# Delta loop over two steps with the next solve between halves of the chunk products, and 64 identity products ahead of it

## What is computed

```python
x = _layernorm(x + _L0_attn_ref(x, ...), axis=-1)   # delta rule
x = _layernorm(x + _L0_ffn_ref(x, ...), axis=-1)
x = _layernorm(x + _L1_attn_ref(x, ...), axis=-1)
x = _layernorm(x + _L1_ffn_ref(x, ...), axis=-1)

def step(S, xs):                                    # one chunk of one head
    qc, kc, vc, bc = xs
    kb = kc * bc[:, None]
    A = jnp.tril(kb @ kc.T, -1)
    U = solve_triangular(eye + A, vc * bc[:, None] - kb @ S, lower=True)
    o = qc @ S + jnp.tril(qc @ kc.T) @ U
    return (S + kc.T @ U, o)
```

## Time and profile before

| | us |
|---|---|
| median of 3 runs | 882.79 |
| lowest and highest | 877.17 and 887.01 |
| the profiled execution | 882.23 |
| its span, first to last instruction | 880.5 |

### The profile page before, as it was taken

One profiled execution on the slowest core, in us unless ns is written; L12 is line 12 of the kernel. 1 busy time (PEld: TensorE's weight loads), 2 busy tenths in 40 slices (PEclk: granted clock), 3 DMA queues, 4 the chain that ended last, 5 costly groups with the idle time before them and its releaser, 6 DMA issues. The chain is left out here.

```text
span 880.5 us, 38401 instructions
## 1 busy us (share of the span) xinstructions
PE 637.1 (72%) x15895; PEld 474.7 (54%) x15895; DVE 440.9 (50%) x1380; ACT 323.9 (37%) x743; POOL 330.2 (38%) x605
## 2 busy tenths in 40 slices
PE   5777105888886875368876189999832899999991
PEld 4565104777775774268876056767621354445551
DVE  3664350223232238826556036676538376776762
ACT  4554100122221213245554036455220556565651
POOL 3577302122121750345675654210021344646442
PEclk9888555599998577669999579999955899999995
DMA  3000222112210900544453111000005333333420
GB/s 104 8 15 21 79 86 69 38 66 71 72 65 22 330 26 1 99 137 131 152 158 106 48 38 28 17 4 4 4 1 99 101 98 100 108 99 106 100 83 1
DMA packets 62384, 63.72 MB, mean 72 GB/s; under 512 B 12432, under 2 KB 51903, under 8 KB 62017
## 3 DMA queue, kind: packets, MB, share of 16 engines
q1 hardware_dynamic: 57056, 52.35, 19.4%
q0 software_dynamic: 5216, 9.87, 5.3%
HBM read 20.50 MB, written 11.93 MB: 37 GB/s over the span
## 5 line engine op out<-in xcount | busy, mean ns | idle before, releaser
L1976 PE MATMUL e_psH<-wac,e_xT 128*64 x184 | 91.1, 618 | 1.0 <-ACT e_xT L2036 0.7
L1978 PE MATMUL e_psH<-e_up_w,e_xT 128*64 128x512 f32 x184 | 91.1, 618 | 0.0
L1921 POOL DMA_INDIRECT e_row<-xe_dram,e_read_at x46 | 44.6, 969 | 69.6 <-DVE spare L2167 44.3
L1926 POOL DMA_INDIRECT out<-spare,e_write_at x46 | 46.5, 1011 | 48.1 <-ACT spare L2053 37.8
L577 POOL TENSOR_TENSOR tb<-tinv,mb 128x128 f32<-128x128 f32 x64 | 24.3, 401 | 106.8 <-PE d_psY L594 106.8
L1321 ACT ACTIVATE e_hT<-e_psH,e_b 128x128 f32<-128x128 f32 x156 | 44.5, 369 | 39.2 <-PE e_psH L1277 39.2
L1233 POOL DMA_INDIRECT e_row<-xe_dram,e_read_at x39 | 38.7, 993 | 42.1 <-DVE spare L1392 27.7
L1277 PE MATMUL e_psH<-e_xT,e_up_w 128*128 128x128 f32 x312 | 45.5, 293 | 12.0 <-issue 9.9
L1997 PE MATMUL e_psY<-vb,e_hT 128*64 x368 | 50.9, 282 | 2.9 <-issue 2.9
L2160 DVE TENSOR_TENSOR e_h<-e_pre,e_psH 128x512 f32<-128x512 f32 x46 | 31.6, 688 | 42.4 <-ACT e_pre L2042 42.4
L2000 PE MATMUL e_psY<-e_down_w,e_hT 128*64 128x128 f32 x368 | 50.9, 282 | 0.0
(11 more groups left out here) (369 smaller groups left out, 1749.0 us busy)
## 6 DMA issues: line engine op xcount, KB each, us to landing
e_down_w<-vb SPq DMA_DIRECT2D x92, 128.0 KB, 2.0
e_up_w<-wa SPq DMA_DIRECT2D x39, 256.0 KB
xe_dram<-xe SPq DMA_DIRECT2D x2, 2080.0 KB, 12.4
vk_now<-vk SPq DMA_DIRECT2D x16, 192.0 KB
kq_now<-kq SPq DMA_DIRECT2D x16, 192.0 KB, 2.1
outs_dram<-spare SPq DMA_DIRECT2D x39, 64.0 KB
r<-in_L_attn_hidden_states SPq DMA_DIRECT2D x8, 256.0 KB, 3.1
gk_now<-gk SPq DMA_DIRECT2D x16, 128.0 KB, 2.0
```

The source lines that it names most:

```text
L1921: pool.indirect_dma_start(out=row[g % ROWS][:, :], out_offset=None, in_=x_dram, in_offset=bass.IndirectOffsetOnAxis(ap=read_at[:, g:g + 1] ...
L1926: pool.indirect_dma_start(out=out, out_offset=bass.IndirectOffsetOnAxis(ap=write_at[:, g:g + 1], axis=0), in_=z[:, g], in_offset=None, bou ...
L1976: nc.tensor.matmul(psH[g % 2][0:HALF, j], xT[g % 2][:, 0:HALF], wac[:, bass.ds(who[0][j], 1)].rearrange("p a f -> p (a f)"), start=True, s ...
L1978: mm = nc.tensor.matmul(psH[g % 2][HALF:P, j], xT[g % 2][:, HALF:P], up_w[g % 2][j][:, :], start=True, stop=True)
```

## The change

PE's loop now covers two steps in a pass, with buffers by the parity of the step, and has 7 passes. A step starts the solve of the step after it: the three bursts of the solve of t + 1 and the serial chain of t - 1 stand between the two halves (one sequence each) of the chunk products of t. `scan` is split into `states` and `outputs`, and the outputs are issued one place later. There are six identity products a step instead of nine. Step 0 and half of step 1's solve stand ahead of the loop, the rest of step 14, step 15 and its scan behind it. `mt`, `qe` and `kq_now` have two buffers, and the two banks psY and psZ become `psY[0]` and `psY[1]`; `across` writes to the bank that `first` has written, after ACT's copy. 24 identity products stand at the start of the delta stage, 40 at the end of the inversion's PE list, after a wait for `turned`, which counts the inversion's last two copies.

```diff
@@ stage_invert, PE
                 mm.then_inc(l_ps, 1)
+                pe.wait_ge(turned, SU)
+                half_words = sb["ident"][:, :].bitcast(BF16)[:, 0:P]
+                for i in range(40):
+                    nc.tensor.matmul(psW[:, i % 4], half_words, half_words, start=True, stop=True)
@@ stage_delta, buffers
-        vk_now, kq_now, gk_now = tmp("vk_now", [P, B * H, RW]), tmp("kq_now", [P, B * H, RW]), tmp("gk_now", [P, B * H, CH])
+        vk_now, gk_now = tmp("vk_now", [P, B * H, RW]), tmp("gk_now", [P, B * H, CH])
+        kq_now = [tmp(f"kq_now{i}", [P, B * H, RW]) for i in range(2)]
-        mt, qe = tmp("mt", [P, NC, B, CH]), tmp("qe", [P, B, NC, CH])
+        mt, qe = ([tmp(f"{n}{i}", s) for i in range(2)] for n, s in (("mt", [P, NC, B, CH]), ("qe", [P, B, NC, CH])))
-        solved_in, crossed_in = bank("d_psY", [P, 512]), bank("d_psZ", [P, 512])
+        solve = [bank(f"d_psY{i}", [P, 512]) for i in range(2)]
@@ stage_delta, SP
-                    if t:
-                        sp.wait_ge(c_ps, t)
+                    if t >= 2:
+                        sp.wait_ge(c_ps, t - 1)
@@ stage_delta, PE
+                def step(t, i, loads):
+
+                    j = 1 - i
+                    first(t + 1, j)
+                    states(t - 1, 0, j)
+                    per_chunk(t, 0, i, loads)
+                    full_array(rest[i])
+                    outputs(t - 1, 0, j)
+                    states(t - 1, 1, j)
+                    across(t + 1, j)
+                    outputs(t - 1, 1, j)
+                    states(t - 1, 2, j)
+                    per_chunk(t, 1, i)
+                    outputs(t - 1, 2, j)
+                    states(t - 1, 3, j)
+                    full_array(rest[i])
+                    second(t + 1, j)
+                    outputs(t - 1, 3, j)
-                pe.wait_ge(const, 3)
-                first(0, True)
-                across(0)
-                second(0)
-                per_chunk(0, True)
-                with pe.Fori(1, PER) as t:
-                    first(t, False)
-                    scan(t - 1, 0)
-                    full_array(rest[1])
-                    across(t)
-                    scan(t - 1, 1)
-                    full_array(rest[0])
-                    second(t)
-                    scan(t - 1, 2)
-                    full_array(rest[1])
-                    scan(t - 1, 3)
-                    per_chunk(t, False)
+                for _ in range(8):
+                    full_array(rest[1])
+                pe.wait_ge(const, 1)
+                first(0, 0, True)
...
+                with pe.Fori(0, PER // 2 - 1) as m:
+                    step(2 * m + 1, 1, 16 * m + 16)
+                    step(2 * m + 2, 0, 16 * m + 32)
...
@@ stage_delta, ACT
+                solved(0)
+                crossed(0)
+                for t in range(PER):
+                    if t + 1 < PER:
+                        solved(t + 1)
+                        crossed(t + 1)
+                    own(t)
@@ stage_delta, DVE
+                for t in range(PER + 1):
+                    if t < PER:
+                        remainders(t)
+                    if t >= 2:
+                        outputs(t - 2)
...
```

More of the change, by code:

```diff
@@ L568, in _ @@
                 pool.memset(S[:, 0], 0.0).then_inc(const, 1)
-                pool.memset(mt[:, :, :, :], 0.0).then_inc(const, 1)
+                for i in range(2):
+                    pool.memset(mt[i][:, :, :, :], 0.0).then_inc(const, 1)
                 pool.memset(uw[:, :], 0.0).then_inc(const, 1)
@@ L587, in full_array @@
                     for _ in range(3):
-                        nc.tensor.matmul(bank[:, :], half_words, half_words, start=True, stop=True)
+                        nc.tensor.matmul(bank, half_words, half_words, start=True, stop=True)
                 def apply(i, right, out, done):
@@ L611, in across, with second @@
                         for c in range(NC):
-                            mm = nc.tensor.matmul(psZ[row(c), bh], gk_now[key(c), bh], y0[key(c), bh * RW:(bh + 1) * RW], start=True, stop=True)
+                            mm = nc.tensor.matmul(psY[i][row(c), bh], gk_now[key(c), bh], y0[key(c), bh * RW:(bh + 1) * RW], start=True, stop=True)
                     mm.then_inc(z_ps, 1)
-                def second(t):
+                def second(t, i):
                     pe.wait_ge(expanded[1], t + 1)
@@ L618, in second @@
                     pe.sem_inc(passed, 1)
[L619 to L642, removed]
@@ L644, in scan, with per_chunk @@
-                def scan(t, c):
+                    apply(1, lambda bh: zz[:, bh * RW:(bh + 1) * RW], psY[i], w_ps)
+                def per_chunk(t, b, i, loads=0, start=False):
+                    if b == 0:
+                        pe.wait_ge(kq_in[i], loads)
+                        if not start:
+                            pe.wait_ge(on_done, t)
+                            pe.wait_ge(mt_done, t)
+                            pe.wait_ge(qe_done, t)
+                        pe.wait_ge(uw_done, t + 1)
+                        pe.sem_inc(passed, 1)
+                    for h in range(H):
+                        bh, at = b * H + h, (b * H + h) * RW
+                        for c in range(NC):
+                            nc.tensor.matmul(psC[row(h), c, b * P:b * P + RW], uw[row(c), at + DV:at + DV + CH], kq_now[i][row(c), bh],
+                                             start=True, stop=True)
+                        for c in range(NC):
+                            nc.tensor.matmul(psC[row(h), c, b * P + RW + CH:b * P + RW + 2 * CH], uw[row(c), at:at + DV], kq_now[i][row(c), bh, DK:RW],
+                                             start=True, stop=True)
+                        for c in range(NC):
+                            mm = nc.tensor.matmul(psC[row(h), c, b * P + RW:b * P + RW + CH], kq_now[i][row(c), bh, 0:CH], uw[row(c), at:at + DV],
+                                                  start=True, stop=True)
+                    if b == B - 1:
+                        mm.then_inc(c_ps, 1)
@@ L646, in scan, with states @@
+                def states(t, c, i):
                     pe.wait_ge(s_sb, NC * t + c + 1)
@@ L651, in scan, with outputs @@
                         for h in range(H):
-                            mm = nc.tensor.matmul(psS[row(h), b], mt[key(h), c, b], S[key(h), c, b], start=True, stop=True)
+                            mm = nc.tensor.matmul(psS[row(h), b], mt[i][key(h), c, b], S[key(h), c, b], start=True, stop=True)
                     mm.then_inc(s_ps, 1)
+                def outputs(t, c, i):
                     if c == 0:
@@ new lines, in _ @@
+                across(1, 1)
+                per_chunk(0, 1, 0)
+                full_array(rest[0])
+                second(1, 1)
+                with pe.Fori(0, PER // 2 - 1) as m:
+                    step(2 * m + 1, 1, 16 * m + 16)
+                    step(2 * m + 2, 0, 16 * m + 32)
+                t = PER - 1
+                states(t - 1, 0, 0)
+                per_chunk(t, 0, 1, 16 * PER // 2)
+                outputs(t - 1, 0, 0)
+                states(t - 1, 1, 0)
+                per_chunk(t, 1, 1)
@@ L680, in _, with solved @@
+                outputs(t - 1, 1, 0)
+                for c in range(2, NC):
+                    states(t - 1, c, 0)
+                    outputs(t - 1, c, 0)
                 for c in range(NC):
-                    scan(PER - 1, c)
+                    states(t, c, 1)
+                    outputs(t, c, 1)
             @block.scalar
             def _(act):
-                for t in range(PER):
+                def solved(t):
                     act.wait_ge(y_ps, t + 1)
```

87 lines of the change are left out of this document (53 added, 34 removed).

## The result

The changed kernel takes 1018.95 us (median of four executions, 1018.06 to 1019.88) and the kernel before, measured beside it, 881.67 us (877.17 to 887.01): a ratio of 1.155, interval 1.149 to 1.162. The prediction said 1019.0. The experiments ran on two other chips, on both of which the kernel before takes 920 to 922 us (the changed one takes 1060 on the second); each is compared with the kernel before on its own chip. The first chip ran the doubled loop, the one-step loop with six identity products and the two kernels with identity products taken out or put in, the second all others. The 41 us by which the changed kernel is slower there lie behind the delta stage: its last copy of `on` starts at 410.64 us in the first trace and at 410.58 in the other.

A forecast was written before the change was run, and what follows sets the result against it. It took PE's code fetching, 3.81 us per 256-instruction block, as the bound on the changed delta loop; first pass, six passes and tail end the stage 136.6 us later: 882.2 + 136.6 = 1018.8, said as 1019 us, range 872 to 1040.

The forecast's parts named there:

- The likeliest case: Delta loop: the two-step body overflows PE's code store, every block is refetched each pass; 1019 us, chance 0.55.
- How long the code is: Delta stage: 2113 instructions a pass touch 9 blocks, a tenth fetched ahead; 1216 instructions before the loop, 909 behind.
- First pass: Delta loop's start: 3250 instructions of new code from 137.1 us, 12.7 blocks, 48.4 us, ending at 185.5 us.
- Six more passes: Delta loop after its first pass: 9 blocks at 3.81 us plus 2.1 us, 36.4 us each, 218.6 us together.
- Tail: Behind the delta loop: 3.25 blocks of new code, 13.5 us against 4.3 before, ending at 417.6 us.
- 40 and 24 identity products: Inversion's end and ahead of the delta loop: cost 0 each; up to 1.8 us for the 24 left to the range.
- PE's idle time in the stage: Sign in the delta stage that the forecast is right: PE's idle time up by about 130 us.
- Clock: Delta stage: the 24 products may raise PE's clock, worth up to 2.6 us, nothing where PE waits for code.
- Reordering hidden: Delta loop: new order, second psY bank and doubled buffers count 0, as 36 us passes cover every wait between engines.
- the rival "held": Delta loop: all ten blocks stay held, no refetching, 6.7 us a step; 881 us (868 to 888), chance 0.30.
- collisions only: Delta loop: only colliding blocks are refetched, four at 3.81 us a pass, 27 us a pass; 962 us, chance 0.13.
- Fetching costs nothing: Delta stage: code fetches are hidden, so it takes 114 us instead of 146.4; 850 us in all, chance 0.02.

The follow-up runs named there:

- doubled loop: The kernel before with its loop body written out twice, order, buffers and waits unchanged, no identity products added: 1051.22 us, ratio 1.140 to the kernel before.
- one-step loop with six identity products: The changed kernel with one step a pass, single kq_now, mt and qe, one psY for the solves: four executions of 924.00 to 957.91 us, no ratio given.
- padded loop of 1560 instructions: The kernel before with 249 small identity products (32 x 32) added at the end of its loop body: 1043.54 us, 1.133 of the kernel before, one execution.

## Why the prediction was right, and where it was not

The likeliest case came in, for the reason given: the body of two steps is refetched in every pass, at a block per 3.8 us. That 1018.95 meets 1019 this closely is luck: the four terms below are off by 1.4 to 2.4 us each, with both signs. By its steps (predicted, measured):

- *How long the code is.* 9 or 10 packets a pass and about 140 in all; 10 and 140. The 288 products ahead of the loop are step 0 and the whole solve of step 1, all three bursts (the description of the change says half of it). The store's size, left open between six blocks and ten, is eight with the one ahead.
- *First pass*: ends at 185.5 us; 183.80. The 3250 instructions went a little faster than a block per 3.81 us.
- *Six more passes*: 6 x 36.4 = 218.6 us; 183.80 to 403.8, 220.0 us. The turn costs about a full block, as assumed: PE has nothing for 3.6 to 4.1 us at the six turns.
- *Tail*: 13.5 us; the last outputs end at 419.19 + 0.42 = 419.6, 15.8 us behind the loop. Sum of the stage: 138.6 us instead of 136.6.
- *Rest of the kernel*: assumed unchanged; 2.4 us less behind the stage (1016.7 - 419.6 against 880.5 - 281.0). Its cause was not followed. With the +2.0 it makes the total look better than the terms are.
- *40 and 24 identity products*: 0, and so they are in the kernel before. In the changed kernel the time is 6 to 11 us less with them, by the two traces because they push the loop's start away from an edge. The forecast counted their instructions only as a shift of the first edge and did not ask how many blocks the body touches from another start. The time did not suffer by it, since the start with the products was the one computed.
- *PE's idle time in the stage*, a sign that was named: up by about 130 us; 26.0 (146.51 - 120.47) to 114.1 (285.11 - 171.00), up by 88. The sign forgot that PE's own work takes longer at the half clock: its busy time in the stage rose by 50.5 us. The sum doesn't use it.
- *Clock*: the step "24 identity products" left up to 2.6 us open for it where PE does not wait for code. PE never got there: 0.50 through the whole loop. A step at half clock without refetching takes 10.26 us (one-step loop), so two are 20.5. By that, an estimate, of the 21 us by which a pass is longer than 15.7 a bit under 5 would be lost to the clock at this level even if all code were held, and 16 to the code alone.
- *Reordering hidden*: right to 1.4 us a pass (36.5 against 35.1 in the doubled old order). But the term of the rival "held" was mis-sized: 6.7 us a step. With one bank and one step a pass it is 7.72. By that step its time would have been above the 881 us given; the second bank and a turn every other step may give back a part, which no run shows.
- *Rivals*: "collisions only" asks for four packets a pass and 962 us; nine or ten came in each of the kernels over the limit. "Fetching costs nothing": refuted by all of them. "All held" is what bodies of seven blocks show, not one of nine.

## What to carry to other kernels

Count TensorE's instructions of a loop body (an f32 product here is four: two loads and two matmuls) and the 256-instruction blocks that they touch from where the body starts; with the one fetched ahead more than eight meant in every kernel here that each pass pays some 3.8 to 4.1 us for each block touched (30.74 / 8, 39.0 / 10, 36.5 / 9), in the old order and in the new. A loop that is unrolled to overlap more must stay within that. Over the limit, the code ahead of the loop made 2.4 us a pass by shifting its start; that it can also put a body on one or the other side of the limit follows from the count and was not run. PE idle "<-issue" at a steady beat in the middle of equal matmuls, with one packet of q8 to each, is the sign; the groups that wait for PE only show its shadow.

## What the hardware did unexpectedly

- A store of eight blocks gives no part of a loop back that needs nine with the one ahead: 200 packets at 1820 instructions a pass, 74 at 1560.
- A loop jumps back four blocks and fetches nothing as long as all is held (before). The Trainium skill, "Runtime: NRT & Kernel Launch", section Instruction fetch mechanics, has a taken branch wait for a fetch when its target is outside the current window of two pages; these rows don't agree.
- PE can be 95% busy (58.45 of 61.78 us) with small products and stay at 1.2 GHz: so in the trace of the one-step loop with six identity products a step, while the same loop with nine had 2.4 GHz from 174.5 us on. The two differ in those three products alone, but ran on different chips, and one execution with six, of which there is no trace, had a mean clock of 0.825. In the kernel before and the one with the first step in the loop, the clock rose only after the last wait for code had ended: end at 162.94 and rise at 175.5 us, 150.02 and 163.5. Why the padded loop of 1560 instructions changed its clock back and forth (0.69 in the pass shown) is open.
